# Graph attention's prologue in a new order, and self-loops added on VectorE

## The reference, cut to what matters

```python
x = layernorm(x + gcn(x, src, dst, edge_weight))        # relu(segment_sum(w * (x W)[src]) + b)
x = layernorm(x + gat(x, edges + self-loops))           # this stage, 4 heads of 32
x = layernorm(x + dot_attention(x, edges))
x = layernorm(x + sage(x, edges))

# gat, for each head
e = leaky_relu(a_s[src] + a_d[dst], 0.2)
m = segment_max(e, dst);  p = exp(e - m[dst]);  z = segment_sum(p, dst)
out = segment_sum(h[src] * p / (z[dst] + 1e-16), dst) + bias + x @ skip_W + skip_b
out = (out - mean) * rsqrt(var + 1e-5) * ln_g + ln_b
```

## Time and profile before

| | us |
|---|---|
| median of 3 runs | 2183.96 |
| lowest and highest | 2182.42, 2190.05 |
| the profiled execution, its own time | 2186.22 |
| its span in the profile | 2184.5 |
| main part, from the first span on VectorE (588.69) to its last weigh (1485) | 896 |
| one lap of the loop (start of one issue of loads, 755.06, to the next, 826.35) | 71.3 |
| graph attention's prologue, from the last sum of the first layer (532.6) to the first span | 56 |

### The profile page before, as it was taken

How to read it: one execution, slowest core, us unless ns; L and a number is a source line. 1 busy time by engine, 2 the same in 40 slices (tenths; PEclk the granted TensorE clock), 3 DMA queues, 4 the chain that set the end, 5 groups by cost and what they waited for, 6 DMA issues and landing times. The chain is left out here.

```text
span 2184.5 us, 45557 instructions
## 1 busy us (share of the span) xinstructions
PE 1849.6 (85%) x17150; PEld 1417.9 (65%) x17151; DVE 1736.4 (79%) x1784; ACT 1199.1 (55%) x2210; POOL 118.8 (5%) x221
## 2 busy tenths in 40 slices
PE   3666776998788988888888888894999999899997
PEld 2666665544566766776667666674688888755655
DVE  5999998001599999999999999977688888677376
ACT  1566666001577677776777677765666666500202
POOL 4000000100000000000000000000000000011010
PEclk9999999999999999999999999985999999999999
DMA  4799999999044124421443044324355555299294
GB/s 115 221 267 265 266 267 260 256 272 239 1 122 123 42 82 122 122 65 58 122 122 97 28 121 122 93 63 105 77 121 120 120 120 150 91 363 404 82 402 172
DMA packets 483056, 341.89 MB, mean 157 GB/s; under 512 B 323176, under 2 KB 475008, under 8 KB 476336
## 3 DMA queue, kind: packets, MB, share of 16 engines
q1 hardware_dynamic: 478640, 337.64, 55.6%
q0 software_dynamic: 720, 1.77, 0.3%
q10 hardware_dynamic: 3632, 1.61, 0.3%
HBM read 214.05 MB, written 126.94 MB: 156 GB/s over the span
## 5 line engine op out<-in xcount | busy, mean ns | idle before, releaser
L1128 ACT ACTIVATE exponentials<-gr_ps,att_cols 128x256 f32<-128x256 f32 (+1 forms) x1300 | 485.8, 491 | 181.0 <-PE gr_ps L983 178.9
L983 PE MATMUL gr_ps<-ident,gr_r 128*128 128x128 f32 (+1 forms) x2500 | 370.5, 287 | 41.3 <-DVE gr_r L1329 39.4
L1016 PE MATMUL gr_ps<-exponentials,heads 128*33 128x128 f32 (+1 forms) x5000 | 369.2, 283 | 34.9 <-DVE exponentials L1335 34.9
L1335 DVE SCALAR_TENSOR_TENSOR exponentials<-exponentials,gr_count_t 128x3072 f32<-128x3072 f32 (+1 forms) x104 | 344.2, 3310 | 25.8 <-ACT exponentials L1128 24.8
L983 PEld LDWEIGHTS gr_ps<-ident,gr_r 128*128 128x128 f32 (+1 forms) x2500 | 275.4, 145 | 123.3 <-issue 103.5
L1297 DVE CUSTOM_DVE_ANT_0 gr_unread<-gr_src_rows,gr_closed 128x3125 bf16<-128x3125 f32 (+1 forms) x100 | 341.3, 3413 | 17.2 <-ACT gr_src_rows L1182 12.5
L1016 PEld LDWEIGHTS gr_ps<-exponentials,heads 128*33 128x33 f32 x5000 | 259.1, 115 | 103.0 <-issue 50.8
L585 PE MATMUL bm_ps<-bm_hot 128*96 128x100 bf16 x4224 | 224.7, 210 | 98.2 <-DVE bm_hot L535 97.2
L585 PEld LDWEIGHTS bm_ps<-bm_hot 128*96 128x96 bf16 x4224 | 207.4, 124 | 115.8 <-DVE bm_hot L535 115.8
L619 ACT ACTIVATE bm_stage<-bm_ps 96x800 f32<-96x800 f32 x264 | 211.7, 831 | 111.8 <-PE bm_ps L585 90.3
L535 DVE TENSOR_TENSOR bm_hot<-bm_hot,near 128x2304 bf16<-128x2304 bf16 x132 | 179.2, 1358 | 18.9
(11 more groups left out here) (310 smaller groups left out, 1967.4 us busy)
## 6 DMA issues: line engine op xcount, KB each, us to landing
adjacency<-bm_stage SPq DMA_DIRECT2D x264, 300.0 KB, 3.5
count_pair<-adjacency SPq DMA_DIRECT2D x37, 1600.0 KB, 8.7
count_more<-count_by_source SPq DMA_DIRECT2D x30, 1600.0 KB, 8.3
count_by_source<-gr_count_t SPq DMA_DIRECT2D x12, 3200.0 KB, 17.2
count_pair<-count_by_source SPq DMA_DIRECT2D x20, 1600.0 KB, 8.5
gr_src_rows<-adjacency SPq DMA_DIRECT2D x18, 1600.0 KB, 15.0
count_more<-adjacency SPq DMA_DIRECT2D x13, 1600.0 KB, 8.5
gr_count_t<-adjacency SPq DMA_DIRECT2D x5, 1600.0 KB, 15.1
```

Source lines behind the costliest of these rows:

```text
L983: last = pe.transpose(ps[:, i % RINGS, c:c + n], r[0:n, slot(g, h) + j, s * P:(s + 1) * P], k.ident[0:n, 0:n])
L1016: last = pe.matmul(ps[j * PAIR:j * PAIR + C + 1, 7, 0:rows(g)], heads[:, h, s, :], e[:, s, c:c + rows(g)], start=s == 0, stop=s == NT - 1, ...
L1128: last = act.activation(e[:, s, places(g, h)], ps[:, i % RINGS, c:c + w], ACT.Exp, bias=cols[:, h, s:s + 1])
L1335: dve.scalar_tensor_tensor(part, part, 1.0, count_t[:, first:last, places(g, 0)], ALU.min, ALU.mult).then_inc(weighed, 1)
```

## The change

1. **Self-loops.** GpSimd's additions in super-tiles 1 to 12 are gone. VectorE does them in `add_own(g + 1)`, in head 1, after its last `best` and ahead of `weigh_first(g, 1)`. GpSimd still does the two of super-tile 0.
2. **Prologue of graph attention.** `source_rows` comes in the three groups of the layer norm, heads 0 and 1 right behind the turned x and ahead of `mix`. The rows of heads 2 and 3 are no longer products: TensorE transposes att_cols with each column read 128 times, and ScalarE scales by 4. Both masks and the first 24 blocks of counts of super-tile 0 are done during the layer norm.
3. **Super-tile 0** has an order of its own on VectorE (`first_super`): three of the maxima of heads 2 and 3 ahead of the first weighing, and two of super-tile 1 later. Its masks for super-tile 1 move from head 1 to head 2.
4. **Prologue of dot-product attention.** The sum of the two bias vectors moves into the stage before. VectorE normalises 4 of the 12 tiles of the first group; `gain` is split, so that `centre(1, 0)` stands ahead of `add_old(1)`; VectorE takes the second part of turned x (`take_last`); only one query product stands ahead of the second turn.

The diff, cut:

```diff
@@ gcn_gat_rows @@
+        PLACES = (((0, 0, 3), (1, 3, 3), (2, 6, 3), (3, 9, 3)), ((4, 12, 3), (5, 15, 3), (6, 18, 2)),
+                  ((7, 20, 3), (3, 23, 2)))
+        TURNED = ((0, 12), (12, 25))
+        BY_PRODUCT = 2
+        ADDED = (2, 6)
+        EARLY_BANKS = (((0, 3, 0),), ((3, 2, 0), (7, 1, 8)))
...
@@ gpsimd @@
             pool.memset(r[:, :, N:NP], 0.0).then_inc(padded, 1)
-            with pool.Fori(1, LAST - 1) as g:
-                super_tile(g)
-            super_tile(LAST - 1)
-            super_tile(LAST)
@@ tensor @@
+            def early_counts(j):
+                pe.wait_ge(looped, j + 1)
+                pe.wait_ge(normed, ADDED[j])
...
+            def turn_rows(h, half):
+                for t in range(*TURNED[half]):
+                    b, c = tile_columns(t)
+                    last = pe.transpose(ps[:, b, c:c + P], cols[:, h, t:t + 1].to_broadcast([P, P]), k.ident[:])
                 last.then_inc(rows_made, 1)
...
+            for j in range(TWO):
+                early_counts(j)
+            pe.wait_ge(taken_n, 1)
             turn_x(0)
             pe.wait_ge(spread, 1)
+            source_rows(0, 0)
+            pe.wait_ge(taken_n, TWO)
+            turn_x(1)
+            turn_x(2)
+            source_rows(0, 1)
+            source_rows(0, 2)
+            for n in range(len(GROUPS)):
+                source_rows(1, n)
+            pe.wait_ge(rows_kept, rows_parts(1) + 2)
             mix(0)
...
@@ scalar @@
+            mask(0, 0)
             deviate(0)
-            mask(0, 0)
+            take_early(0)
+            mask(0, 1)
+            take_early(1)
+            deviate(1)
             take_x(0)
-            deviate(1)
-            take_heads(0)
-            take_x(1)
             deviate(2)
             keep_rows(0, 0)
+            take_x(1)
             take_x(2)
             keep_rows(0, 1)
-            mask(0, 1)
-            take_heads(1)
-            take_heads(2)
+            keep_rows(0, 2)
...
@@ vector @@
+            def add_own(g):
+                for j in range(width(g)):
+                    dve.wait_ge(loaded[j], g * 16 + 16)
+                    own = count[:, j, bass.ds((g * TWO + j) * P, P)]
+                    dve.tensor_tensor(own, own, k.ident[:], ALU.add).then_inc(looped, 1)
+
+            def first_super():
...
+                level(0, 0)
+                span(0, 0)
+                best(0, 2, 0)
+                best(0, 2, 1)
+                best(0, 3, 0)
+                weigh_first(0, 0)
+                span(0, 1)
+                best(0, 3, 1)
+                level(0, 1)
+                weigh_rest(0, 0)
+                weigh_first(0, 1)
+                span(0, 2)
+                weigh_rest(0, 1)
+                add_own(1)
+                weigh_first(0, 2)
+                span(0, 3)
+                weigh_rest(0, 2)
+                best(1, 0, 0)
+                best(1, 0, 1)
+                weigh_first(0, 3)
...
             def super_tile(g):
...
                     if width(g2) > 1:
                         best(g2, h2, 1)
+                    if h == 1:
+                        add_own(g + 1)
                     if h % TWO:
                         weigh_first(g, h)
@@ attend_rows, vector @@
             measure_norm(1)
+            normalise_old(ACT_OLD, GROUPS[0][1])
             centre(0, 1)
             gain(0)
+            add_old(0)
             measure_norm(0)
             gain(1)
             centre(1, 0)
+            add_old(1)
             measure_norm(1)
             centre(1, 1)
             finish_norm(1)
+            take_last()
@@ attend_rows, tensor @@
             turn_x(0)
-            queries(0)
+            pe.wait_ge(xt_out, 1)
+            query(0)
             turn_x(1)
-            pe.wait_ge(query_out, 3)
-            pe.wait_ge(xt_out, NG)
+            pe.wait_ge(xt_last, 1)
             score(0, 0, 0)
-            queries(1)
+            for b in range(1, NCW):
+                query(b)
             score(0, 0, 1)
```

More of the change, by code:

```diff
@@ L962, in mix @@
                 for b, first, tiles in PLACES[n]:
+                    if first == PLACES[2][1][1]:
+                        pe.wait_ge(heads_out, 1)
                     for i in range(tiles):
@@ L1171, in super_tile @@
                         take_counts(g, 2)
-                    if h == 1 and not is_super(g, LAST):
+                    if h == (2 if is_super(g, 0) else 1) and not is_super(g, LAST):
                         for j in range(width(g + 1)):
@@ L1348, in weigh_rest @@
                 weigh(g, h, CUT, NT)
+            def add_own(g):
[4 more added lines that the diff above has]
+            def first_super():
+                for h in range(TWO):
+                    for j in range(TWO):
+                        best(0, h, j)
+                level(0, 0)
[18 more added lines that the diff above has]
+                weigh_first(0, 3)
+                best(1, 1, 0)
+                best(1, 1, 1)
+                level(1, 0)
             def super_tile(g):
@@ L1354, in super_tile @@
                         weigh_rest(g, h - 1)
-                    elif not is_super(g, 0):
+                    else:
                         weigh_rest(g - 1, HEADS - 1)
@@ L1568, in turn_x, with query @@
                 last.then_inc(x_turned, 1)
-            def queries(n):
-                pe.wait_ge(xt_out, n + 1)
-                for b in CHUNKS[n]:
-                    if b == 7:
-                        pe.wait_ge(query_out, 4)
-                    pe.matmul(ps[:, CHUNK_BANK[b], 0:CW], joint[:, 0], k.XT[:, b * CW:(b + 1) * CW], start=True, stop=True
-                              ).then_inc(query_made, 1)
+            def query(b):
+                if b > 3:
+                    pe.wait_ge(query_out, b - 3)
+                pe.matmul(ps[:, CHUNK_BANK[b], 0:CW], joint[:, 0], k.XT[:, b * CW:(b + 1) * CW], start=True, stop=True
+                          ).then_inc(query_made, 1)
             def make_values(j):
@@ L1712, in deviate, with normalise_tiles @@
                                ).then_inc(root_ready, 1)
-            def normalise_tiles(layer, n, dst, ready):
+            def normalise_tiles(layer, n, first, end, dst, ready):
                 act.wait_ge(mean_ready, layer * len(GROUPS) + n + 1)
-                for t in range(*GROUPS[n]):
+                for t in range(first, end):
                     last = act.activation(dst[:, t], T[:, t], ACT.Identity, scale=norm.root[:, t:t + 1],
@@ L1779, in begin_sums @@
             def begin_sums():
-                steps.step(dve.tensor_tensor(k.vecs[:, 0], k.vecs[:, 0], k.vecs[:, 1], ALU.add))
                 dve.tensor_scalar(inv[:, :, 0:NT - 1], node[:, :, :, C], 1e-16, None, ALU.add)
@@ L1818, in centre, with normalise_old @@
                                          ).then_inc(mean_ready, 1)
+            def normalise_old(first, end):
+                dve.wait_ge(mean_ready, 1)
+                for t in range(first, end):
+                    last = dve.tensor_scalar(T[:, t, :], T[:, t, :], norm.root[:, t:t + 1], norm.mean[:, t:t + 1],
+                                             ALU.mult, ALU.add)
+                steps.step(last)
             def gain(n):
```

121 lines of the change are left out of this document (69 added, 52 removed).

## The result

The changed kernel takes **2223.68 us** (median, 2216.17 to 2224.31), the kernel before 2183.19 on the same chip: a ratio of 1.0167, 95% interval 1.0151 to 1.0184. It is slower. The forecast was 2221 in a range of 2208 to 2238. The profiled execution took 2223.29, with a span of 2221.6, 37.1 over that of before.

The account below looks back on a forecast made before the run. VectorE was taken to bound graph attention's loop, busy 98%. Terms 51.7 - 3.9 - 7.3 - 3.3 = +37.2 us on a span of 2184.5 gave 2221.7, forecast as 2221 us, range 2208 to 2238.

Parts of the forecast that it names:

- The stall in the loop: Loop, head 1: VectorE waits at its additions for the second load; with the additions themselves, +51.7 us over ten laps.
- The second addition: Loop, head 1: each lap's second addition comes behind the stall and costs VectorE 0.29 us, 2.9 in all.
- the question whether the issue would move up: Loop: load issue hangs on VectorE's head 0, 21.4 us after lap start, so the wait repeats in every lap.
- GpSimd's contention: Loop: without GpSimd's additions, `weigh_first` regains 0.25 and `span` 0.14 us, 0.39 a lap, -3.9.
- The larger figure: Loop: if VectorE lost a whole GpSimd operation each time, 9.2 us would come back instead of 3.9; not adopted.
- Graph attention's prologue: Up to the loop's start: first `span` 10.3 us earlier, at 578.4, less 3.0 from new waits: -7.3, bounds 0 and 18.
- The waits in super-tile 0: Super-tile 0, from `weigh_rest(0, 0)` on: waits of 1.1, 3.5, 1.7 and 2.5, 8.8 us, against 5.4 and 0.8 before.
- Dot-product attention's prologue: Before that stage's first minimum: first scores some 5 us earlier, 3.3 of the wait remain; -3.3, bounds 0 and 6.
- A: Rival, 15%: in the loop, TensorE's clock falls after the stall, 1.7 us a lap comes through; +17, 2238 us.
- B: Rival, 12%: the second load lands in time, no wait at the loop's additions; -8.7, 2175 us, down to 2155.
- C: Rival, 8%: both prologues bring nothing, the loop alone is left; +47.8, 2232 us.

Follow-up runs that it names:

- run 3: Changed kernel with the loop's two additions moved behind `weigh_first(g, 1)` and `level`, later in VectorE's order: 2183.66 us, 0.9988 of the kernel before.
- run 4: Changed kernel with the two additions moved ahead of both maxima of head 1, earlier in VectorE's order: 2299.74 us, 1.0516 of the kernel before.
- run 5: Changed kernel with the next super-tile's two loads issued ahead of the store of the last head's sums: 2202.62 us, 1.0085 of the kernel before.
- run 6: Changed kernel with the edits of run 3 and run 5 together: 2176.89 us, 0.9951 of the kernel before.
- run 7: Run 1 with one more 128x128 addition on GpSimd in each lap, into a buffer nobody reads: 2179.19 us, one execution.
- run 8: Run 1 with super-tile 0 in VectorE's old order and super-tile 1's masks in head 1, new prologue kept: 2169.02 us, 0.9924 of the kernel before.
- run 1: Changed kernel with the loop's additions given back to GpSimd, prologues kept: 2176.76 us, 0.996 of the kernel before.
- run 9: Kernel before with only the new prologue of dot-product attention (part 4): 2183.81 us, 0.9994 of the kernel before.
- maxima_and_loads: Run 8 with the loads ahead of the store and the additions on GpSimd: 2171.07 us, 0.9926 of the kernel before.
- run 2: Kernel before with only the loop's additions moved to VectorE in head 1, ahead of `weigh_first` (part 1): 2234.64 us, 1.0227 of the kernel before.
- all_late: Run 8 with the additions on VectorE, late, and the loads ahead of the store: 2167.17 us, 0.9905 of the kernel before.

## Why the prediction was right

The mechanism was right: one term makes the loss, and it is the stall. That the sum fits the spans to 0.1 us (+37.2 against +37.1) is luck: the loop's terms were 47.8 (51.7 - 3.9) and measured 48.0, the prologues gave 0.7 and 0.8 less than forecast, and 1.8 us that nobody forecast went the other way.

**The stall in the loop, +51.7 predicted.** Right in mechanism, place and nearly in size. From the point of VectorE to the second load I had 48.8 us over ten laps, or 45.9 behind the first addition; 44.6 were measured. The second addition costs 0.21 and not 0.29 (769.59 to 769.80), since the next instruction starts before its end. Runs 3, 4 and 5 confirm the reason: the place moved by +4.2 and -6.9 us changes the lap by -3.9 and +7.2, the issue moved by -1.9 changes it by -1.8. The step that carried the forecast was the question whether the issue would move up once VectorE is held. It hangs on head 0, the stall is in head 1, and so it repeats: 21.4 us behind the lap's start in the kernel before, in the changed one and in run 4.

**GpSimd's contention, -3.9.** Right: 3.35 and 3.73 came back, and run 6 shows laps equal to those with GpSimd. With the stall, the second addition and this, the lap is 71.28 + 0.29 + 4.28 + 0.21 - 0.39 = 75.67, measured 75.71. The larger figure that I worked out from the Trainium skill, 9.2, was wrong, and run 7 shows why. The Trainium skill, "SBUF — State Buffer", section "Who interferes with whom", says that who comes first keeps the port for the whole instruction and the other is blocked. In run 7 VectorE's `weigh_first` starts at 761.21, the extra addition behind it, and the loser is GpSimd, 3.51 instead of 0.46; VectorE loses 0.14 (`span`) to 0.25 (`weigh_first`) at each meeting in these runs. The trace agrees with the rule; I had given the loss to the wrong engine.

**Graph attention's prologue, -7.3.** Measured -6.6. The first `span` was forecast at 578.4 and stands at 577.61, the loop's at 655.0 and stands at 655.72; but the layer ahead of it ended 0.5 earlier in this execution. The waits in super-tile 0 were counted as 8.8 and are 10.0: none ahead of `weigh_first(0, 1)` where I had 1.1, then 6.0, 1.4 and 2.6 where I had 3.5, 1.7 and 2.5. Of the 2.5 us by which the 6.0 was missed, 1.5 go with the clock. TensorE's interleave ahead of it, which waited 4.3 us for `weigh_rest(0, 0)`, takes 9.2 us (606.31 to 615.50) and not the 7.7 that I took over, at a granted clock of 0.57 at its start:

```profile
606.00:610.00 4.00, 3.69 (x24) 2.46 (x24) 3.52 (x2) 0.84 (x2) 0.00 (x0) 0.57 1.30 273
```

The step count was sound but for that. What I did not ask is what the new prologue would be worth with the old order of the super-tile: the answer, run 8, is about twice as much, some 13.

**Dot-product attention's prologue, -3.3.** The trace of the changed kernel has -2.5, the mean over eleven executions of the new code -2.0, or -2.3 with the sum of the biases. Here the first score starts 5.5 nearer to the stage's start, but the first minimum only 4.1, not 5: that score took 4.34 us instead of 2.92, the granted clock being 0.50 for part of it:

```profile
1580.00:1582.50 2.50, 2.50 (x5) 1.23 (x4) 0.11 (x1) 0.00 (x0) 0.00 (x0) 0.50 0.00 0
```

Before, TensorE had two more query products between its long pause and this score, and the clock was 1.00. But the order alone does not decide: in run 1, with the same code, the score took 2.95 at a clock of 1.00, and the 1.4 us between are the whole step from a wait of 3.31 to one of 4.70. The clock was no part of my sum.

**The rivals.** A (the clock makes the stall dearer): the clock does fall in each lap, and VectorE has no wait from it in any lap; the gathers, up to 5.3 us, have a `span` and a `weigh_rest` beside them, 3.73 + 3.62. Run 4 shows the same with twice the stall. B (no stall): wrong in the change as it was made, but runs 3 and 6 show how near it was; 4.2 us further down the queue 0.5 a lap is left of the wait, and with the loads ahead of the store 0.3 in the first lap alone. C (prologues bring nothing): refuted by run 1.

**The -1.8 behind the second minimum** need not be an effect of the change. From there to the end of the span it is 631.0 to 631.6 us in the changed kernel, runs 3, 4, 5 and 9 and `maxima_and_loads`, and 632.5 to 633.5 in the kernel before, runs 1, 2, 6, 7 and 8 and `all_late`. The code behind the second minimum is the same in all, and kernels with the new prologue have either value; but the two with the old one both have the larger, and one trace of each kernel does not settle it. **Left open** is which event in TensorE's clock or elsewhere sets the one or the other value, and with it the scatter of the first score.

## What to carry to other kernels

A wait belongs to the place in an engine's queue, not to the operation: before work is moved to the engine that sets the time, put the landing time of its input beside the point in the lap at which the engine will ask, and move the work down the queue until the input is there. Where cover is filled by work taken from later, look at what that work was covering there, and do the sum again when another part of the same change shortens the wait that was to be filled. And undo a change part by part, in both directions: here one median hid a loss of 8 us behind a gain of some 13 in the same stage.

## What the runs showed of the hardware that I had not expected

- An addition on GpSimd that starts behind a long VectorE instruction with two operands in SBUF takes about as long as the rest of this: 3.51 us instead of 0.46. VectorE lost 0.14 to 0.25 at each meeting, with one or two additions on GpSimd.
- Behind a pause of TensorE of 6 us the gathers took 4.2 to 5.3 us in all ten laps, the granted clock being 0.50 for part or all of them; behind one of 1.5 us, in the kernel before, 2.8 in four laps and 4.1 to 4.5 in six. Neither kernel had a wait of VectorE from it.
- Two 128x128 additions in a row take 0.49 us on VectorE, one 0.29; between `level` and `span` the two lengthened the lap by 0.40.
